# Two of eight expert matrices turned in the first attention chunk, one rounding step moved to another engine, and the borders and the tail written in another order

## What is computed

```python
x = x + tanh(g_xattn[0]) * L0_xattn(layernorm(x), ctx)        # attention over 154 context rows
x = x + tanh(g_ffn[0])   * L0_ffn(layernorm(x), Wg, Wu, Wd)   # 8 experts, all on every token
x = x + tanh(g_xattn[1]) * L1_xattn(layernorm(x), ctx, ...)   # 8 heads of 64, then Wout
x = x + tanh(g_ffn[1])   * L1_ffn(layernorm(x), wg, W, b)     # routed, below
# L1_ffn: each token goes to the expert e with the highest of 8 probabilities, if e has
# fewer than 256 tokens before it; out = gate * (token @ W[e].T + b[e])
```

## Time and profile before

| | |
|---|---|
| median of 3 runs | 1211.69 us (1211.50 to 1212.44) |
| the profiled execution, its own time | 1211.75 us |
| its span | 1209.9 us |
| PE busy | 1193.1 us (99%) |
| DVE busy | 1043.4 us (86%) |
| POOL busy | 886.5 us (73%) |
| ACT busy | 746.5 us (62%) |

### The profile page before, as it was taken

How to read it: one execution, slowest core, us unless ns; L and a number is a source line. 1 busy time by engine, 2 the same in 40 slices (tenths; PEclk the granted TensorE clock), 3 DMA queues, 4 the chain that set the end, 5 groups by cost and what they waited for, 6 DMA issues and landing times.

```text
span 1209.9 us, 18394 instructions
## 1 busy us (share of the span) xinstructions
PE 1193.1 (99%) x6122; PEld 982.9 (81%) x6122; DVE 1043.4 (86%) x1737; ACT 746.5 (62%) x1541; POOL 886.5 (73%) x847
## 2 busy tenths in 40 slices
PE   9999999999999999999999999999999999899998
PEld 7788888888888888888888888888888878788876
DVE  6877899999999999999999999999999975577656
ACT  5775566666666666666666666666666546476644
POOL 5656688888888888888888888888888726445535
PEclk9999999999999999999999999999999999999999
DMA  4022100000000000000000000000000320001121
GB/s 144 27 97 72 52 27 27 27 27 27 27 27 27 27 27 27 27 27 27 27 27 27 27 27 27 27 27 27 27 27 27 122 85 38 19 2 37 36 94 73
DMA packets 42365, 48.27 MB, mean 40 GB/s; under 512 B 4239, under 2 KB 40143, under 8 KB 42015
## 3 DMA queue, kind: packets, MB, share of 16 engines
q1 hardware_dynamic: 40240, 43.38, 11.0%
q0 software_dynamic: 1440, 3.41, 0.8%
q10 hardware_dynamic: 591, 0.32, 0.1%
HBM read 37.36 MB, written 10.29 MB: 39 GB/s over the span
## 4 chain that ended last, share of the span: by engine, by line
PE 93%; DVE 3%; POOL 1%; issue 1%; ACT 1%; POOLq 0%; DVEq 0%; ACTq 0%
PE bank L1410 26%; PE bank L1412 26%; PE bank L1411 26%; PE bank L1654 2%; PE bank L1664 2%; PE bank L1637 1%; PE bank L1614 1%; PE bank L1846 1%; PE bank L1829 1%; PE bank L1306 1%; PE bank L1370 1%; DVE xn L1913 1%; PE bank L1355 1%; PE bank L1789 1%; PE bank L1608 1%
## 5 line engine op out<-in xcount | busy, mean ns | idle before, releaser
L1410 PE MATMUL bank<-xop_hi,w_hi 128*128 128x512 f32 x896 | 349.2, 390 | 2.3 <-DVE xop_lo L491 1.2
L1412 PE MATMUL bank<-xop_hi,w_lo 128*128 128x512 f32 x896 | 348.6, 389 | 0.0
L1411 PE MATMUL bank<-xop_lo,w_hi 128*128 128x512 f32 x896 | 348.6, 389 | 0.0
L2078 DVE TENSOR_TENSOR hid_lo<-hid,hid_hi 128x512 fp32r<-128x512 f32 x228 | 231.3, 1039 | 6.0 <-ACT hid_hi L1048 6.0
L1410 PEld LDWEIGHTS bank<-xop_hi,w_hi 128*128 128x128 f32 x896 | 168.2, 188 | 38.5 <-issue 1.8
L1412 PEld LDWEIGHTS bank<-xop_hi,w_lo 128*128 128x128 f32 x896 | 168.2, 188 | 34.8
L1411 PEld LDWEIGHTS bank<-xop_lo,w_hi 128*128 128x128 f32 x896 | 168.2, 188 | 34.7
L1048 ACT CAST hid_hi<-hid 128x512 fp32r<-128x512 f32 x228 | 140.9, 623 | 63.6 <-PE bank L1412 38.3
L1032 ACT ACTIVATE s<-bank 128x512 f32<-128x512 f32 x128 | 78.2, 611 | 95.2 <-PE bank L1412 95.2
L1410 PE MATMUL bank<-hid_hi,wd_hi 128*128 128x512 f32 x344 | 134.2, 390 | 0.8 <-DVE hid_lo L2078 0.6
L1412 PE MATMUL bank<-hid_hi,wd_lo 128*128 128x512 f32 x344 | 133.9, 389 | 0.0
(11 more groups left out here) (286 smaller groups left out, 2595.5 us busy)
## 6 DMA issues: line engine op xcount, KB each, us to landing
raw_gu<-in_L_ffn_Wg_dram SPq DMA_DIRECT2D x32, 256.0 KB, 2.7
raw_gu<-in_L_ffn_Wu_dram SPq DMA_DIRECT2D x32, 256.0 KB, 3.0
raw_d<-in_L_ffn_Wd_dram SPq DMA_DIRECT2D x32, 256.0 KB, 3.6
slots<-empty_row SPq DMA_DIRECT2D x1, 2080.0 KB, 10.2
xr<-slots SPq DMA_DIRECT2D x8, 260.0 KB, 5.8
x_res<-in_x_dram SPq DMA_DIRECT2D x4, 512.0 KB, 7.6
x_mid<-x_res SPq DMA_DIRECT2D x1, 2048.0 KB, 8.2
x_res<-x_mid SPq DMA_DIRECT2D x4, 512.0 KB, 5.3
```

Of the source, the lines that this page charges most:

```text
L1410: mm(ps, w, a, start=start, stop=False, skip_group_check=True)
L1411: mm(ps, w, a_low, start=False, stop=False, skip_group_check=True)
L1412: return mm(ps, w_low, a, start=False, stop=True, skip_group_check=True)
L2078: nc.vector.tensor_tensor(out=hid_lo[n % 2][h][:], in0=hid[h][:], in1=hid_hi[n % 2][h][:].bitcast(F32), op=ALU.subtract).then_inc(lo_ready ...
```

## The change

The edits, in the order of the program:

- Chunk 0: matrices 1 and 0 are turned on PE at two places where it has a wait before, into banks 7 and 5, which nobody uses there; DVE copies them behind the reciprocals `dens(0, 0, 1)` and `dens(0, 1, 1)`. PE waits for the copies before it uses bank 5 (`attend`) and bank 7 (`project`).
- `late_bias_rest` goes from POOL, where it stood at the border of chunks 0 and 1, to DVE. The branch that calls it is that of a chunk without routing, so it stands in chunk 0, behind `dens(0, 2, 1)`.
- Borders: POOL's power for `xn4` comes ahead of all four scatters of the chunk (before, one scatter was ahead of it).
- Chunk 3: matrices 2 and 3 take the place of 0 and 1. On DVE the reciprocals `dens(3, 3, 1)` and the variances of the early tiles come ahead of `route_counts`, and the early tiles are normalised ahead of `route_slots`.
- Tail: matrix 4 alone ahead of `locations`, matrix 5 between `late_transposes(0)` and `dense(0)`; `dense(6)` comes behind unit 12 in place of 10; `dense(7)` is written as two products of 256 columns, in banks 7 and 4, each signalled by itself.

```diff
-    WE_PS, EARLY_WE = (2, 0), (0, 1)
-    DENSE_PS = (4, 6, 5, 7)
+    WE_PS, EARLY_WE, FIRST_WE = (2, 0), (5, 7, 0, 1), (1, 0)
+    DENSE_PS, LAST_DENSE_PS = (4, 6, 5, 7), (7, 4)
-    DENSE_AFTER = {2: 4, 6: 5, 10: 6, 15: 7}
+    DENSE_AFTER = {2: 4, 6: 5, 12: 6}
...
                 if front:
                     x_low(c + 1)
+                    power(LN_ROUTE, CT, c + 1)
                 if route:
-                    scatter(c - 1, range(1) if front else range(CT))
-                if front:
-                    power(LN_ROUTE, CT, c + 1)
-                if c == 0:
-                    late_bias_rest()
-                    pool.wait_ge(consts_ready, 8)
-                if route and front:
-                    scatter(c - 1, range(1, CT))
+                    scatter(c - 1)
...
+                if c == 0:
+                    expert_matrix(FIRST_WE[0])
                 if route:
                     logits(r, (0, 1, 2))
                 scores_after_exps(c, 1, (0,))
                 if route:
                     logits(r, (3,))
+                if c == 0:
+                    expert_matrix(FIRST_WE[1])
...
-            for e in range(2, 4):
-                expert_matrix(e)
+            expert_matrix(4)
             locations(NC - 1, EARLY, 0, LAST_LOC)
             project(NC - 1, CT - 1)
             late_transposes(0)
+            expert_matrix(5)
             dense(0)
-            for e in range(4, 6):
-                expert_matrix(e)
             dense(1)
...
+            def last_dense():
+
+                j, g = LATE[-1], E // 2 - 1
+                pe.wait_ge(c_res, NT + 1)
+                for i, b in enumerate(LAST_DENSE_PS):
+                    e = 2 * g + i
+                    if i == 1:
+                        pe.wait_ge(late_dve, LATE_DVE[DENSE // 2])
+                    mm(bank[b][:, 0:D], both[:], be_hl[:, e * D:(e + 1) * D], start=True, stop=False)
+                    for k in range(KB):
+                        ins = mm(bank[b][:, 0:D], xn4T[:, k, j * P:(j + 1) * P], weT[:, e, k, :], start=False, stop=k == KB - 1)
+                    ins.then_inc(late_ps, 1)
...
                 if with_route:
                     route_choice(r)
+                else:
+                    late_bias_rest()
                 maxes(c, 3, 1)
                 dens(c, 3, 0)
                 add_attention(c, 1)
+                if not with_front:
+                    row_norms(r)
                 pT_out(c, 2, 1)
-                if not with_front:
-                    route_counts(r)
-                    row_norms(r)
-                    route_variances(c, EARLY)
                 dens(c, 3, 1)
                 if with_front:
                     front_normed(f)
+                else:
+                    route_variances(c, EARLY)
                 if with_route:
                     route_places(r)
                 if not with_front:
+                    route_counts(r)
+                    route_normed(c, EARLY)
                     route_slots(r)
-                    route_normed(c, EARLY)
                     add_attention(c, 2)
```

More of the change, by code:

```diff
@@ L823, in late_bias_rows @@
                 nc.gpsimd.tensor_copy(be_hl[:], be_all[0:LO + 1, :, :].rearrange("p e d -> p (e d)")).then_inc(consts_ready, 1)
[L825 to L831, removed]
             def chunk(c, front, route):
@@ L1703, in expert_matrix @@
                 n = len(WE_PS)
+                if e == FIRST_WE[0]:
+                    pe.wait_ge(we_in, 16 * (E + 1))
                 if e >= len(EARLY_WE) + n:
@@ L1720, in chunk @@
                 else:
-                    pe.wait_ge(we_in, 16 * (E + 1))
-                    for e in range(len(EARLY_WE)):
+                    for e in range(len(FIRST_WE), len(EARLY_WE)):
                         expert_matrix(e)
+                if c == 0:
+                    expert_matrix(FIRST_WE[0])
                 if route:
@@ L1731, in chunk @@
                 else:
-                    pe.wait_ge(e_wT, 1)
+                    pe.wait_ge(e_wT, 3)
                 p_transposes(c, 0, (0,))
                 scores_after_exps(c, 1, (1,))
+                if c == 0:
+                    pe.wait_ge(e_wT, 1)
                 attend(c, 0, (0,))
@@ L1874, in _ @@
                     dense(DENSE_AFTER[u])
+            last_dense()
         @block.vector
@@ L2287, in route_choice, with late_bias_rest @@
                                         op=ALU.is_equal).then_inc(r_one, 1)
+            def late_bias_rest():
+                dve.wait_ge(consts_ready, 7)
+                row = slice(LO, LO + 1)
+                nc.vector.tensor_tensor(out=be_hl[row, :], in0=be_all[row, :, :].rearrange("p e d -> p (e d)"),
+                                        in1=be_hl[row, :].bitcast(F32), op=ALU.subtract).then_inc(consts_ready, 1)
             def route_counts(r, of=range(CT)):
@@ L2352, in add_late_experts @@
                 ps = bank[DENSE_PS[i % len(DENSE_PS)]]
+                second = ps[:, D:2 * D]
                 route.did(nc.vector.scalar_tensor_tensor(out=x, in0=ps[:, 0:D], scalar=share[:, t, 2 * g:2 * g + 1], in1=x,
@@ L2355, in add_late_experts @@
                 own(route)
-                ins = nc.vector.scalar_tensor_tensor(out=x, in0=ps[:, D:2 * D], scalar=share[:, t, 2 * g + 1:2 * g + 2], in1=x,
+                if i == DENSE - 1:
+                    dve.wait_ge(late_ps, DENSE + 1)
+                    second = bank[LAST_DENSE_PS[1]][:, 0:D]
+                ins = nc.vector.scalar_tensor_tensor(out=x, in0=second, scalar=share[:, t, 2 * g + 1:2 * g + 2], in1=x,
                                                      op0=ALU.mult, op1=ALU.add)
@@ L2390, in expert_matrix_out @@
             def expert_matrix_out(e):
-                dve.wait_ge(e_wT_ps, e + 1)
+                dve.wait_ge(e_wT_ps, e + 1 if e not in FIRST_WE else FIRST_WE.index(e) + 1)
                 nc.vector.tensor_copy(weT[:, e, :, :].rearrange("p k d -> p (k d)"), bank[EARLY_WE[e]][:]).then_inc(e_wT, 1)
@@ L2403, in chunk @@
                 else:
-                    expert_matrix_out(0)
+                    expert_matrix_out(2)
                 maxes(c, 1, 0)
                 dens(c, 0, 1)
+                if c == 0:
+                    expert_matrix_out(FIRST_WE[1])
                 if with_front:
@@ L2417, in chunk @@
                 dens(c, 1, 1)
+                if c == 0:
+                    expert_matrix_out(FIRST_WE[0])
                 if with_front:
```

12 lines of the change are left out of this document (6 added, 6 removed).

## The result

The changed kernel takes **1203.55 us** (median of 4 runs, 1203.11 to 1204.18) against 1211.64 for the kernel before beside it (4 runs, 1211.50 to 1212.44). The ratio is 0.9932, 95% interval 0.9915 to 0.9949: 8.1 us faster. The forecast was 1203.2, in a range of 1202.2 to 1205.2. The profiled run took 1203.55, its span is 1201.6, and 1209.9 before.

What follows compares the result with a forecast made beforehand. PE, busy in 99% of the span, bounds the kernel, so only its waits or work can shrink. Terms sum to 8.4 us, 8.6 with overlaps; 8.5 taken from 1211.7 gives 1203.2 us, range 1202.2 to 1205.2.

Steps and rivals of the forecast that it cites:

- Border 0 to 1: First chunk border: without POOL's bias instruction holding DVE, `xn` takes 1.38 and PE's wait and low clock go; 5.3 us.
- rival D: First border: `xn` is long for another reason, such as the x_res transfer, so 5.3 stays; 1208.5 us, chance 0.05.
- Borders 1 to 2 and 2 to 3: Later borders: POOL's power ahead of the scatters starts 0.8 earlier, removing PE's waits of 0.45 and 0.25; 0.8 us.
- Two matrices in chunk 0, the bias on DVE: Chunk 0: transposes fit PE's waits of 0.7, the 2.2 us bias fits DVE's 2.59 us pause; cost 0.
- rival B: Chunk 0: bias on DVE not free, held by POOL's product or too long; 1204.1 to 1205.1 us, chance 0.16.
- The end of chunk 3: End of chunk 3: DVE's reciprocals and variances come earlier, so PE's wait for the early `xn` goes; 0.6 us.
- The tail: Tail: two matrices fewer on PE and matrix 5 in the `xn4T` wait, less waits uncovered; 1.1, taken as 1.0 us.
- rival C: Tail gives nothing because expert rows from `slots` or DVE's routing chain are late there; 1204.5 us, chance 0.1.
- The last units: Kernel end: split last product and `dense(6)` behind unit 12 end DVE's and POOL's last stores sooner; 0.6 to 0.7 us.
- the smaller of the two paths counts: Kernel end: DVE's `x_res` store gains 0.5, POOL's last store 0.6, both ending together; taken as 0.6 to 0.7 us.
- E: Chunk 0: single-partition bias many times slower on DVE, making the kernel slower than before; 1212.6 us at 12 us, chance 0.03.

Runs made afterwards that it cites:

- bias_back: Changed kernel with the low part of the bias back on POOL at the first border, behind the power: 1209.58 us, ratio 0.9979.
- bias_only: Kernel before with only the low part of the bias moved from POOL to DVE in chunk 0: 1206.18 us, ratio 0.995.
- bias_pool_late: Changed kernel with the bias on POOL again, started only when DVE has written `xn`: 1203.42 us, ratio 0.9927.
- bias_behind_maxes: Changed kernel with the bias one place later on DVE, behind the maxima of tile 3: 1205.65 us, ratio 0.9945.
- chunk3_old: Changed kernel with DVE's old order at the end of chunk 3: 1204.33 us, ratio 0.9935.
- matrices_old: Changed kernel with expert matrices turned as before, 0 and 1 in chunk 3, 2 to 7 in the tail: 1204.27 us, ratio 0.9934.
- dense6_10: Changed kernel with `dense(6)` behind unit 10 again, last dense product still in two: 1208.05 us, ratio 0.9963, profile disturbed elsewhere.
- last_units_old: Changed kernel with `dense(6)` behind unit 10 and the last dense product whole, as before: 1206.79 us, ratio 0.9952, profile disturbed elsewhere.

## Why the prediction was right

By its own steps, forecast first and the trace's account second:

- **Border 0 to 1: 5.3, 5.46.** Right in mechanism, size and clock. `bias_back`, `bias_only` and `bias_pool_late` show that it was POOL's instruction beside DVE's, and rival D is refuted: same transfer, same border, `xn` 1.39. `bias_back` undoes this edit alone and gives 5.6.
- **Borders 1 to 2 and 2 to 3: 0.8, 1.13.** Right in mechanism, too small. A window without a wait is 4.25 long, where I had subtracted the waits and come to 4.47. I had the term 1.0 "with the overlap" and didn't take it: where PE does not stop, its next instruction starts under the end of the last, and a wait costs 0.2 more than the idle time that is shown.
- **Two matrices in chunk 0, the bias on DVE: 0, 0.00.** 2.28 for a forecast of 2.2, 0.28 of the pause left. The Trainium skill (VectorE: DVE Perf Modes, "The TRN2 errata") gives 2.29 for it, an estimate by its formula, and the trace agrees. In rival B DVE would have been the one held. POOL was, with 3.31 us for 1.21, and so it is in all nine profiles with the bias at this place. But the argument against B did not carry this: it said that DVE is at its instruction first, by 0.16. The product's record came 0.04 behind, and in the earlier trace rows POOL's record starts 0.04 behind DVE's too, and there it is DVE that is held. That this side of B did not come true owes something to luck. `bias_behind_maxes` shows what B's price rests on, the chain without slack: 2.1 to 2.3 for 2.28.
- **The end of chunk 3: 0.6, 0.79**, and 0.8 in `chunk3_old`. The same overlap as at the borders is a likely part of the rest (not shown).
- **The tail: 1.0, 0.93**, so rival C is refuted; `matrices_old`, with those of chunk 0 undone too, lost 0.7 by medians, 0.9 by spans, and 0.9 in the stretch of the tail.
- **The last units: 0.6 to 0.7, 0.05.** This is the term that was mis-sized, the step "the smaller of the two paths counts". I took for granted that DVE's last store and POOL's last store both bound the end and are independent, so that 0.5 on one and 0.6 on the other give the smaller of them. The end lies 1.51 behind the landing of POOL's store in both kernels, so only POOL counted, and it came only 0.29 sooner, of which 0.24 went to the landing. The 0.6 for POOL failed at DVE: it takes up unit 13 at 1193.78, 22.88 behind unit 0's first transpose, for 23.18 before, so 0.30 sooner. It stands 1.07 us idle for the product of `dense(6)`, and its adds end only at 1193.69, directly ahead of unit 13. Experts 11 and 12 now also wait for DVE, since units 10 to 12 follow each other with the adds of `dense(5)` between them; what these waits cost was not separated. The weight loads of the two experts in the changed kernel (timeline of PEld):

```profile
1187.02 0.73 PEld L1850 LDWEIGHTS bank<-weT,xeT 128*128 128x128 f32 x4 [0.20 <-DVE ye L2388]
...
1189.51 0.73 PEld L1850 LDWEIGHTS bank<-weT,xeT 128*128 128x128 f32 x4 [0.29 <-DVE ye L2388]
```

- **E** is refuted by the 2.28.

The terms as put sum to 8.4 (8.6 with the overlaps, and the forecast took 8.5), and the account to 8.20: 0.5 more at the borders, 0.2 more in chunk 3, 0.1 less in the tail, 0.65 less at the end, and the 0.16 from ahead of chunk 0. That the total came within 0.4 us owes something to luck, by errors of both signs. `bias_pool_late` is level with the changed kernel; no version here beats it.

## What to carry to other kernels

Where an instruction of VectorE is several times longer than its neighbours of the same shape, look at what GpSimd runs beside it before you look for a transfer: the remedy can be as small as letting one wait for the other, on the same engine. A wait of TensorE cost more than its idle time here, by about 0.2 us each (0.67 for 0.45, 0.44 for 0.25, 1.92 for 1.7), and where the clock fell behind it, in two profiles after only 0.6 us of waiting, another 1.3 to 1.6 (5.46 - 3.9 - 0.2, and 2.14 for 0.59 at the two places of `dense6_10` and `last_units_old`). At the very end of a kernel count to the landing of each transfer and ask which of them the end follows: 0.5 us off the store of `x_res` gave nothing, since the end followed the other store.

## What was not expected of the hardware

- The hold between the two engines goes both ways and covers nearly the whole of the other's instruction: 4.53 us of GpSimd on one partition hold the first of four instructions of VectorE (the four take 5.69 for 1.39), 2.38 hold it so that they take 3.54, and 2.28 us of VectorE hold GpSimd's product for 3.31 instead of 1.21. The Trainium skill (SBUF — State Buffer, "SBUF: two separate sides") says that whichever starts first holds the other for its whole instruction. The lengths agree. The order can't be read from the records: in all three cases VectorE's starts 0.04 us ahead, and in the first two it is VectorE that is held. So two starts as close as that don't tell who will be held; a pause or a semaphore has to keep the two apart.
- One row of 2048 columns costs VectorE 2.28 us, and GpSimd 4.53 to 4.54, whether VectorE has `xn` to write at that time or has written it.
- The length of a wait did not by itself decide about the clock. It stayed at 1.00 behind two waits of 1.7 us in a profile, and was lower behind waits of 3.9 (0.87 over the window), 2.1 (0.63) and, in two of four profiles with the same wait at the same place, 0.6 (0.57).
- On one chip the profiles of all four kernels of a job had DVE and ACT stand still for 1.4 and 3.6 us at the same two places, for a releaser that the trace does not show; on two other chips none of eight profiles had.
